# A two-layer transformer kernel in split float32r: other SBUF addresses for the tiles that TensorE reads

## The reference

```
x = x + L0_attn(layernorm(x))   # 3 heads of width 256, mean over the heads, then @ fc_w.T + fc_b
x = x + L0_ffn(layernorm(x))    # up/gate/down with ternary weights, 1024 wide, silu(up) * gate
x = x + L1_attn(layernorm(x))   # 16 heads of width 128, causal, biases, softmax, W_O
x = x + L1_ffn(layernorm(x))    # int8-quantised tokens @ int8 weights, rescaled, + bias
```

## The kernel before

| Tiles | Held by | Streamed by | Phase before | Phase after |
| --- | --- | --- | --- | --- |
| XT | scores0, values0, project_v | project_y, up_gate, project_qk | 128 | 128 |
| Y, GF (one tile set each, hi and lo) | GF: project_y | scores0, values0 | 96 | 320 |
| E0 / V0 | attend0 / - | - / attend0 | 96 / 96 | 128 / 320 |
| T_up, T_gate / T_down | up_gate / - | - / down | 96 | 320 |
| HID | down | - | 96 | 128 |
| Q / K_parts | scores / - | - / scores | 96 / 96 | 128 / 320 |
| V / PT | attend / - | - / attend | 96 / 96 | 128 / 320 |
| Z | project_out | - | 96 | 128 |
| W and WO, even pairs | W: project_qk | project_v, project_out | 320 | 320 |
| W and WO, odd pairs | W: project_qk | project_v, project_out | 288 | 320 |

## Time and profile before

### The profile page before, as it was taken

The page is one execution under the profiler, slowest core; times in us unless marked ns, Lnnn a source line. Parts: engine busy times, 40 slices in busy tenths (PEclk is TensorE's granted clock), DMA queues, the critical chain, the costliest instruction groups (busy, mean ns, idle before and its releaser), DMA issues.

```text
span 509.0 us, 8910 instructions
## 1 busy us (share of the span) xinstructions
PE 485.7 (95%) x3020; PEld 433.0 (85%) x3020; DVE 379.8 (75%) x967; ACT 294.7 (58%) x690; POOL 282.1 (55%) x378
## 2 busy tenths in 40 slices
PE   8999999999999977899999999999999989999973
PEld 7888998899888866789989989899999979899961
DVE  2676786775756578788878878788888896667887
ACT  2356336535554646676676667676776766655643
POOL 1344234322655456786676777677786796512253
PEclk9999999999999999999999999999999999999998
DMA  8900000000010016665665664755655655000002
GB/s 281 369 23 2 1 0 1 0 1 1 24 41 1 0 41 169 183 178 143 178 176 137 187 177 108 213 177 150 183 168 158 189 149 145 12 1 1 2 0 82
DMA packets 54380, 51.58 MB, mean 101 GB/s; under 512 B 3520, under 2 KB 49728, under 8 KB 54336
## 3 DMA queue, kind: packets, MB, share of 16 engines
q1 hardware_dynamic: 53248, 49.98, 34.1%
q10 hardware_dynamic: 1088, 1.05, 0.6%
HBM read 32.92 MB, written 18.09 MB: 100 GB/s over the span
## 4 chain that ended last, share of the span: by engine, by line
PE 65%; DMA 11%; DVE 11%; ACT 4%; POOL 3%; issue 2%; SPq 2%; DVEq 0%; ACTq 0%
PE bank L390 16%; PE bank L392 16%; PE bank L391 16%; DMA MV<-turned_dram 5%; DMA turned_dram<-BT 4%; PE bank L612 3%; PE bank L613 3%; PE bank L685 2%; PE bank L684 2%; PE bank L683 2%; DMA Wv_sb<-wv 2%; PE bank L623 2%; PE bank L625 2%; DVE SM L1472 1%; POOL PT_lo L1143 1%
## 5 line engine op out<-in xcount | busy, mean ns | idle before, releaser
L1143 POOL TENSOR_TENSOR PT_lo<-MV,PT_hi 128x512 fp32r<-128x512 f32 (+1 forms) x104 | 91.2, 910 | 51.8 <-ACT PT_hi L963 51.4
L952 ACT ACTIVATE PR<-SM,nmax 128x128 f32<-128x128 f32 (+3 forms) x128 | 72.3, 565 | 64.1 <-DVE nmax L1472 63.4
L1088 POOL TENSOR_TENSOR E_lo<-E,E_hi 128x512 fp32r<-128x512 f32 x24 | 31.0, 1298 | 54.9 <-ACT E_hi L876 47.5
L1472 DVE CUSTOM_DVE_ANT_0 SM<-bank,causal 128x384 f32<-128x384 f32 (+3 forms) x102 | 53.9, 529 | 9.3 <-PE bank L685 7.4
L390 PE MATMUL bank<-XT_hi,W_hi 128*128 128x512 f32 x128 | 52.5, 410 | 5.7 <-DVE V_lo L1454 4.1
L963 ACT CAST PT_hi<-MV 128x512 fp32r<-128x512 f32 (+1 forms) x104 | 42.3, 456 | 18.8 <-DMA MV<-turned_dram 18.6
L1491 DVE STREAM_TRANSPOSE BT<-PR 128x128 f32<-128x128 f32 (+1 forms) x104 | 48.1, 491 | 6.5 <-POOL PR L1127 4.8
L392 PE MATMUL bank<-XT_hi,W_lo 128*128 128x512 f32 x128 | 50.6, 395 | 0.0
L391 PE MATMUL bank<-XT_lo,W_hi 128*128 128x512 f32 x128 | 50.4, 394 | 0.0
L391 PE MATMUL bank<-PT_lo,V_hi 128*128 128x128 f32 (+3 forms) x130 | 41.6, 320 | 0.0
L392 PE MATMUL bank<-PT_hi,V_lo 128*128 128x128 f32 (+3 forms) x130 | 41.6, 320 | 0.0
(11 more groups left out here) (186 smaller groups left out, 1606.5 us busy)
## 6 DMA issues: line engine op xcount, KB each, us to landing
MV<-turned_dram SPq DMA_DIRECT2D x104, 160.0 KB, 3.2
turned_dram<-BT SPq DMA_DIRECT2D x26, 384.0 KB, 2.9
stage<-pack SPq DMA_DIRECT2D x32, 256.0 KB, 4.1
turned_dram<-BT SPq DMA_DIRECT2D x26, 256.0 KB, 3.2
X<-x SPq DMA_DIRECT2D x2, 512.0 KB, 8.7
wraw<-wupT SPq DMA_DIRECT2D x1, 1024.0 KB, 10.0
wraw<-wgateT SPq DMA_DIRECT2D x1, 1024.0 KB, 11.8
wraw<-wdownT SPq DMA_DIRECT2D x1, 1024.0 KB, 14.8
```

The costliest lines, as they stand in the source:

```text
L952: act.activation(PR[:, c, 0:(c + 1) * P], SM[:, c % 2, 0:(c + 1) * P], ACT.Exp, bias=nmax1[:, c:c + 1], scale=-1.0, accum_out=sum1[:, c:c ...
L1088: pool.tensor_tensor(E0_lo[:, m, :], E0[:, m, :], E0_hi[:, m, :], ALU.subtract).then_inc(e0_lo, 1)
L1143: pool.tensor_tensor(by_quad(PT_lo[w % 2], c), moved_part(w, c), by_quad(PT_hi[w % 2], c), ALU.subtract).then_inc(mv_lo, 1)
L1472: dve.tensor_tensor_reduce(SM[:, c % 2, 0:n], s_bank(w, c)[:, 0:n], mask, 1.0, HIGHEST, ALU.add, ALU.min, nmax1[:, c:c + 1]).then_inc(s_ma ...
```

## The change

Only addresses. Three unused tiles ("spacers") are declared, and some declarations change places, so that the tiles named above get the phases of the last column: the held tiles of `scores`, `attend`, `project_out`, `attend0` and `down` lie at 128, and what these stream lies at 320. XT stays at 128 and W, T and GF are at 320, so in `project_y`, `up_gate` and `project_qk`, which hold these and stream XT, the two phases stand the other way round. No instruction, wait, shape or order differs: the rows of all engines are the same in both programs but for the line numbers, which move by 11.

```
+PHASES = 512
+MOVING_PHASE = 192
...
+        def spacer(name, nbytes, where=ctx):
+
+            where.enter_context(nc.sbuf_tensor(name, [P, nbytes // 4], F32))
...
         diag = sb("diag", [P, KD, P])

+        spacer("before_moving", MOVING_PHASE + 32)
+
         memt = ExitStack()
         T_up = sb("T_up", [P, KD, DE], F32R, memt)
...
         Y_lo = sb("Y_lo", [P, KD, SEQ], F32R, mem0)
+        V0_hi = sb("V0_hi", [P, CT, D], F32R, mem0)
+        V0_lo = sb("V0_lo", [P, CT, D], F32R, mem0)
         E0 = sb("E0", [P, CT, SEQ], F32, mem0)
+        spacer("before_E0", PHASES - MOVING_PHASE, mem0)
         E0_hi = sb("E0_hi", [P, CT, SEQ], F32R, mem0)
         E0_lo = sb("E0_lo", [P, CT, SEQ], F32R, mem0)
-        V0_hi = sb("V0_hi", [P, CT, D], F32R, mem0)
-        V0_lo = sb("V0_lo", [P, CT, D], F32R, mem0)
...
-        Q_hi = sb("Q_hi", [P, 2, SEQ], F32R)
-        Q_lo = sb("Q_lo", [P, 2, SEQ], F32R)
         K_parts = sb("K_parts", [P, 2, 2, SEQ], F32R)
         K_hi, K_lo = K_parts[:, :, 0, :], K_parts[:, :, 1, :]
-        V_hi = sb("V_hi", [P, V_GROUPS * CT, 2 * DH], F32R)
-        V_lo = sb("V_lo", [P, V_GROUPS * CT, 2 * DH], F32R)
+        PT_hi = [sb(f"PT_hi{i}", [P, CT, SEQ], F32R) for i in range(2)]
+        PT_lo = [sb(f"PT_lo{i}", [P, CT, SEQ], F32R) for i in range(2)]
         SM = sb("SM", [P, 2, SEQ])
         SB = sb("SB", [P, P])
         PR = sb("PR", [P, CT, SEQ])
-        PT_hi = [sb(f"PT_hi{i}", [P, CT, SEQ], F32R) for i in range(2)]
-        PT_lo = [sb(f"PT_lo{i}", [P, CT, SEQ], F32R) for i in range(2)]
+        spacer("before_stationary", PHASES - MOVING_PHASE)
+        Q_hi = sb("Q_hi", [P, 2, SEQ], F32R)
+        Q_lo = sb("Q_lo", [P, 2, SEQ], F32R)
+        V_hi = sb("V_hi", [P, V_GROUPS * CT, 2 * DH], F32R)
+        V_lo = sb("V_lo", [P, V_GROUPS * CT, 2 * DH], F32R)
         memf = ExitStack()
```

## The result

After the change the kernel takes 506.96 us (median of 6 runs, 505.31 to 508.55), beside 509.6 us for the kernel before on the same chip (6 runs, 508.59 to 513.2). The medians lie 2.6 us apart. The ratio of the runs is 0.9943, with a 95% interval of 0.9917 to 0.9969: by it 2.9 us or 0.57% faster, where 5.4 us (1.06%) had been forecast. The time lies inside the range; the gain is about half of the forecast's.

The account below looks back on a forecast made before the run. TensorE was taken as the bound, with 91.6% of layer 0's chain and 61% of layer 1's. Savings of 3.5 x 0.92 and 3.4 x 0.64 gave 5.4 us, from 510.33 to 504.9 us; range 500.5 to 510.5.

Parts of the forecast that it names:

- 115.0 ns with ends at 113.3 and 117.7: Spacing assumed for 256-column matmuls at difference 192: the mean of 32 sequences, its ends the short and long beats.
- scores and attend: Layer 1, difference 0 to 192: savings of 0.75 us at 256 columns, 0.66 at 384 and 0.57 at 512.
- I take the saving per load, 4 ns, and not per column: scores0 in layer 0, 512 columns: each matmul saves 4 ns as its weight load is 128 columns, 0.58 us.
- My lower bound for scores0: scores0 in layer 0: the saving per matmul lies between nothing and 6.5 ns.
- shares of 0.92 and 0.64: Parts of TensorE's saving that reach the end: layer 0 3.2 of 3.5 us, layer 1 2.2 of 3.4.
- The short beat everywhere: Both layers: every sequence at difference 192 keeps the short beat; 8.4 us saved, 501.9 us; chance 0.20.
- The long beat everywhere: Both layers: every sequence takes 117.7 ns; layer 0 wins 1.6 us, layer 1 nothing, 508.8 us; chance 0.14.
- Layer 1 gives nothing back: Layer 1: the probabilities' trip through DRAM bounds each window, so only layer 0 counts; 507.1 us; chance 0.06.
- No effect: All matmuls: two independent read ports, so addresses change nothing; 510.3 us; chance 0.09.
- Slower: Layer 1: turned probabilities meet weight loads on the same DMA queue in six more windows; 517 us; chance 0.07.

Follow-up runs that it names:

- experiment 4: A kernel with TensorE alone, no reference computed: tiles at phases 0 to 480 streamed against one held tile at 0; 256 columns took 113.5 to 119.8 ns by difference.
- experiment 7: The kernel after once more, with no edit; 506.97 us, ratio 0.9951 to the kernel before.
- experiment 8: A kernel with TensorE alone: 256 columns at difference 192 streamed 48 times behind 24 matmuls at each other difference; 113.3 to 113.9 ns or 117.7 to 117.8.
- the five ratios: The kernel after, its repeat, and it with all tiles 32 (twice) and 64 bytes further, against the kernel before: 0.9943, 0.9951, 0.9922, 0.9948, 0.9941.
- experiment 3: The kernel before with W0, W1 and layer 0's tiles moved so that every operand lies at 128, all differences 0; 509.2 us, ratio 0.9989 to the kernel before.

## Why the prediction was right, and where it was not

**That addresses count, and 256 columns at difference 192: right.** The forecast took 115.0 ns with ends at 113.3 and 117.7. The sums, from spacings in the trace after:

| term | forecast us | measured us |
| --- | --- | --- |
| attend0 | 1.38 | 288 x (119.8 - 114.4) = 1.57 |
| down | 0.58 | 128 x (119.5 - 116.0) = 0.45 |
| values0 | 0.58 | 0.59 |
| scores0 | 0.58 | 232.8 before and after: 0 |
| project_y and up_gate | 0.40 | 0.66 |
| project_out, even and odd | 0.60, -0.19 | 0.52, -0.19 |
| project_v, odd and even | 0.63, 0 | 0.51, about 0 |
| scores and attend | 1.98 | 0.46 |
| project_qk | 0.35 | 0.47 |

Those from attend0 to values0, project_out and project_v, all of 256 columns, make 3.58 forecast and 3.45 measured. How project_out and project_v share theirs is chance, since which of them has the short beat differs between executions; that just one of the two has it in nearly every window is why a mean of the two beats was a good forecast for both together.

**The step that failed: "I take the saving per load, 4 ns, and not per column".** No row had 384 or 512 columns at difference 192, and I carried the saving over from 256. Three terms hung on it: scores0 (0.58) and, in scores and attend, 384 columns (0.66) and 512 (0.57), 1.81 us in all. They brought 0, 0.20 and 0. The map of experiment 4 shows why for scores0: at 192 the 512 columns take 233.3 ns, as bad as at most places, and at 224, where Y stood, 233.1. With 384 columns 192 has 174.6 and difference 0 has 174.0. My lower bound for scores0, nothing, was the right value. What 256 columns won in scores and attend was 0.26 us for 0.75: there they stand in threes between other widths and did not take the beats of the long sequences (PT went from 117.7 to 116.6 ns). project_y, up_gate and project_qk gained more than forecast (1.13 for 0.75): among their 512 columns XT with T_gate went from difference 32 to 64 modulo 256, 233.3 to 229.2 ns, and the map has 233.3 and 229.6.

**What reaches the end.** Of the 4.9 us that streaming saved, 2.6 reached TensorE's last start in one trace; in the second it was 5.0 and 4.5. I had set shares of 0.92 and 0.64. For layer 0 0.92 was too high: the waits took 0.95 and 1.2 of 3.2, so some 0.65 is left; TensorE's new waits for VectorE at the places shown above are part of it. For layer 1 no share can be named from one execution, since its waits vary by about 2 us. Nor could the chain give it. The chain after, from 205 to 445 us, as in the earlier trace rows:

```profile
by line: PE bank L401 23.7%; PE bank L403 22.8%; PE bank L402 22.8%; PE bank L694 4.7%; PE bank L695 4.7%; PE bank L696 4.7%; DMA MV<-turned_dram 3.8%; DMA turned_dram<-BT 3.4%; POOL PT_lo L1154 1.5%; PE bank L689 1.4%; PE bank L705 1.0%; S
...
210.12 5.31 DMA MV<-turned_dram
```

The six TensorE lines that had 61% before have 83% here, and 91% in experiment 7, which is the same program. A share that moves this much without an edit can't price a saving; my reading is that two paths end nearly together and the chain takes now the one, now the other.

**The rivals.** *The short beat everywhere* fell: one attend0 head of six has the long beat, and in experiment 8 the long beat comes with all addresses the same. *The long beat everywhere* fell at once (114.4 in attend0). *Layer 1 gives nothing back* (507.1) gave the number nearest to the 506.96 measured, yet its reason, that the trip through DRAM bounds each window, isn't what was found: the tiles of layer 1 had little to win, 1.7 us of streaming for the 3.4 of the forecast, and alone they bring 0.9 us. *No effect*, which follows from the Trainium skill's pages "TensorE: Matmul & The Clock Gate" (Part 2) and "SBUF — State Buffer" ("Who interferes with whom"), fell: in experiment 4 nothing but TensorE works, and the same matmul takes 113.3 or 119.6 ns by its streamed tile's address. What this speaks against is that TensorE's two reads leave each other alone; whether it ever waits for another engine's reads no run here tests. *Slower* did not come: the median load of MV is 3.2 us as before, and the longest 5.31 for 5.28.

**What the profile after was to show.** attend0 in 5.2 to 5.35 us: 5.22, but 5.42 in one head. Durations of 276 to 280 for attend0 and down: 277, 279. project_out alike for both parities: yes. Busy as before within 1 us: VectorE and GpSimd, while ScalarE has 1.2 less. 512 columns held at 128 at 390 to 392: missed, 395. TensorE's busy sum down by 6 to 8 us: missed, 3.7. Its idle time in layer 1 up by 1 to 2 us: missed, 9.9 us from 175 to 480 us in both traces. The 395 alone would have pointed at the failed step.

**What the time itself proves.** Little: the range of 500.5 to 510.5 held the kernel before (509.6) as well as the forecast. That the effect is there rests on the five ratios and the spacings; that 506.96 fell inside the range doesn't speak for the sum, whose gain was twice the measured one.

## What to carry to other kernels

Where TensorE bounds a kernel of float32r matmuls with a weight load each, read the start-to-start spacing of every pair of operands, and look at their addresses modulo 256 before anything else is blamed; a map measured with TensorE alone costs one kernel, and tells long sequences of one width well and mixed ones poorly. Where a pair of tiles has two beats, read many of its sequences: a single one, or a single execution, can show either. Don't carry a saving from one width to another: the best difference for 256 columns is among the bad ones for 512. Moving one tile can also slow the sequences beside it, as Y did with values0. And take the share of a stretch that reaches the end from more than one execution; part of what TensorE saved came back as waits for VectorE.

## What the runs showed of the hardware

- A float32r matmul of 128 x 256 with its own weight load follows the last at 113.3 to 119.8 ns, by the difference of the streamed and the held tile's address modulo 256 bytes; one of 512 columns at 228.4 to 234.2, one of 384 at 173.1 to 176.7. Even the best, 113.3, is above the 106.7 ns that 256 columns take at 2.4 GHz.
- At difference 192 and 256 columns there are two stable beats, 113.5 and 117.8 ns, with the same tiles and no other engine at work. A sequence mostly keeps the beat it starts with. What picks it is open: the same 24 matmuls ahead of it led to the short beat in one kernel and to the long one in another (behind 160: 113.3 and 117.8; behind 224: 118.3 and 113.9), and two executions of one program differ in it.
- In layer 1 the beats of project_out and project_v are tied: in 22 of 23 windows one is short and the other long, in the kernel after and in its repetition. How the beat passes from one to the other is open.
- The neighbours count: values0 takes 114.6 ns beside a Y at difference 192 and 117.2 beside one at 64, its own addresses unchanged. K_parts and PT in layer 1, where widths alternate, miss the map by some 5 ns at 512 columns (234.0 and 235.1 at 64, where it has 229.6); K_parts took some 232 at difference 0 in the kernel before and 227.6 in experiment 3, where the map has 228.4. Why is open.
- Two executions of one program differ by some 2 us in layer 1's waits while the streaming between them agrees to 0.2 us in each layer.
